# Starting the expert tiles of a routed feed-forward layer while the last rows are still being routed

## What is computed

```python
x = x + tanh(g_xattn[0]) * xattn(ctx_2048, layernorm(x), mask, mask, ...)   # 8 heads of 16
x = x + tanh(g_ffn[0])   * ffn(layernorm(x), ...)
# ffn:
scores = sigmoid(x_flat @ gate.T + bias)             # 2048 tokens x 9 experts
top_scores, selected = top_k(scores, 2)
top_scores = top_scores / (sum(top_scores) + 1e-20)
for e in range(9):
    h = silu(x_flat @ ew1[e].T) * (x_flat @ ew3[e].T)  # 352 hidden
    out = out + cw[:, e:e + 1] * (h @ ew2[e].T)
```

## Time and profile before

| | us |
|---|---|
| median of three runs | 274.59 |
| the profiled execution, its own time | 274.52 |
| its span (first to last instruction) | 272.7 |
| PE busy / DVE / ACT / POOL | 189.9 / 175.5 / 133.8 / 116.7 |

### The profile page before, as it was taken

One profiled execution on the slowest core, in us unless ns is written; L12 is line 12 of the kernel. 1 busy time (PEld: TensorE's weight loads), 2 busy tenths in 40 slices (PEclk: granted clock), 3 DMA queues, 4 the chain that ended last, 5 costly groups with the idle time before them and its releaser, 6 DMA issues.

```text
span 272.7 us, 5842 instructions
## 1 busy us (share of the span) xinstructions
PE 189.9 (70%) x1480; PEld 158.4 (58%) x1481; DVE 175.5 (64%) x681; ACT 133.8 (49%) x383; POOL 116.7 (43%) x196
## 2 busy tenths in 40 slices
PE   0399988989887878766300005999999999999300
PEld 0377745666555645453200004999999999998200
DVE  2248875787998779677685911566776677676125
ACT  1355539888867667573570101355455445544000
POOL 3315741332314651761377700156555655555400
PEclk9999999999999799975555555799999999999955
DMA  5904400094000010180012203022222222220096
GB/s 186 303 20 123 110 0 2 5 324 161 4 1 21 30 33 0 39 287 16 5 54 79 88 20 79 2 54 61 60 62 64 59 52 64 65 56 33 0 257 204
DMA packets 23718, 21.02 MB, mean 77 GB/s; under 512 B 3520, under 2 KB 19844, under 8 KB 23696
## 3 DMA queue, kind: packets, MB, share of 16 engines
q1 hardware_dynamic: 19152, 15.67, 19.8%
q0 software_dynamic: 2432, 4.30, 4.9%
q10 hardware_dynamic: 2112, 0.80, 1.2%
HBM read 14.81 MB, written 6.47 MB: 78 GB/s over the span
## 4 chain that ended last, share of the span: by engine, by line
PE 50%; DVE 21%; issue 9%; DMA 8%; SPq 6%; POOL 3%; ACT 2%; another core or an unknown queue 0%; DVEq 0%; POOLq 0%; ACTq 0%
PE ps_b L1007 10%; PE score_ps L975 5%; PE score_ps L976 5%; PE score_ps L977 5%; DVE mx L672 5%; PE score_ps L831 3%; PE pt_ps L1017 3%; DMA mask_b<-in_mask 3%; PE ps_b L940 3%; PE score_ps L841 3%; DMA w<-y_rows 3%; PE ps_a L919 2%; POOL x_rows L490 2%; PE ps_a L990 2%; DVE st L737 2%
## 5 line engine op out<-in xcount | busy, mean ns | idle before, releaser
L505 POOL DMA_INDIRECT y_rows<-probsT,ids x40 | 39.7, 992 | 11.1 <-POOL ids L503 11.1
L333 ACT ACTIVATE probs<-score_ps,less 128x128 f32<-128x128 f32 x128 | 37.1, 394 | 2.4 <-DVE less L676 2.4
L490 POOL DMA_INDIRECT x_rows<-stage,slot x32 | 33.5, 1047 | 9.8 <-issue 8.6
L1007 PE MATMUL ps_b<-w,probsT 128*128 (+1 forms) x240 | 33.4, 275 | 1.1 <-DVE probsT L808 1.1
L420 ACT COPY probsT<-pt_ps 128x256 f32<-128x256 f32 x40 | 14.9, 372 | 37.1 <-PE pt_ps L1017 31.6
L1007 PEld LDWEIGHTS ps_b<-w,probsT 128*128 128x128 f32 (+1 forms) x240 | 31.6, 190 | 1.7 <-issue 1.6
L484 POOL TENSOR_TENSOR rs<-ve,minus_half 128x1 f32<-128x1 f32 x16 | 9.0, 564 | 53.2 <-DVE ve L742 41.2
L793 DVE TENSOR_TENSOR probs<-probs,score_ps 128x352 f32<-128x352 f32 x40 | 20.9, 522 | 16.9 <-issue 11.5
L975 PE MATMUL score_ps<-w_high,xg_low 128*128 x80 | 30.5, 382 | 0.0
L990 PE MATMUL ps_a<-cst,xg 128*128 128x128 f32 x40 | 11.6, 289 | 26.7 <-DMA xg<-x_rows 25.9
L976 PE MATMUL score_ps<-w_low,xg_high 128*128 x80 | 26.6, 333 | 0.0
(11 more groups left out here) (149 smaller groups left out, 463.4 us busy)
## 6 DMA issues: line engine op xcount, KB each, us to landing
w<-in_w13T SPq DMA_DIRECT2D x3, 1056.0 KB, 8.4
xg<-x_rows SPq DMA_DIRECT2D x40, 65.0 KB
ctx_r<-in_ctxT SPq DMA_DIRECT2D x4, 512.0 KB, 5.0
w<-y_rows SPq DMA_DIRECT2D x8, 256.0 KB, 6.3
w<-in_w2T SPq DMA_DIRECT2D x1, 1728.0 KB
mask_b<-in_mask SPq DMA_DIRECT2D x4, 256.0 KB, 6.2
out<-xs SPq DMA_DIRECT2D x4, 256.0 KB, 3.3
xs<-in_x SPq DMA_DIRECT2D x3, 256.0 KB, 8.8
```

What stands on the lines that cost most here:

```text
L333: last = nc.scalar.activation(probs[:, r % 2, h, :], score_ps[:, r % 2, h, :], ACT.Exp, bias=less[:, r % 2, h:h + 1], scale=SCALE)
L490: pool.indirect_dma_start(x_rows[:, :], bass.IndirectOffsetOnAxis(ap=slot[:, c, p:p + 1], axis=0), stage[:, c, p, :], None, bounds_check=l ...
L505: pool.indirect_dma_start(y_rows[:, :], bass.IndirectOffsetOnAxis(ap=ids[:, r:r + 1], axis=0), yt[:, r, :], None, bounds_check=last_row, o ...
L1007: last = nc.tensor.matmul(bank[7][:, 0:D], hidT[0:cn, q3, c, :], w2[0:cn, bass.ds(e3, 1), c, :].rearrange("p o d -> p (o d)"), start=(c == ...
```

## The change

The numbers in the constants: 40 tiles are now handed out in three parts, `TILES` = 8, 8 and 24. A part is worked out from the rows placed so far: parts 0 and 1 hold only tiles whose 128 rows are all there (after two and after three groups), part 2 the rest.

- `turns` ends after step 16. The end of the attention chain of blocks 14 and 15 and the routing of groups 2 and 3 go between the first eleven tile steps (`between`), on each engine by a list of its own. The first sixteen tile steps are written out.
- The first eight tiles wait for the scatters of groups 0 and 1 only, the next eight for group 2, the rest for group 3. The table is made three times (`table_counts`, `table_rows`, and `table_used`, which takes away the tiles already given).
- A group's scatters are spread: two in step 4g+10, two in 4g+11, four in 4g+12.
- The pads are no longer aimed: all of `x_rows` (19,584 rows of 520 B, 10.2 MB) is filled with pads by one DMA ahead of the scatters, issued on SP behind the weights.
- The first-layer weights are loaded in the projections, into `w13_low`; ACT rounds them to `w13_high` there (seven of nine; two in steps 0 and 1), and DVE subtracts in place, two in the projections and one in each of steps 0 to 6.
- `maxima` is one reduction with its sign turned; the scale moves into `head_rows`. The four blocks' logits stand side by side in PSUM and are read once per group. The second layernorm writes straight into `stage` (with `scalar_tensor_tensor`), POOL makes the second copy (`keep`) and adds the epsilon; ACT no longer copies rows. The residual is kept in place, without a copy.
- In the tiles ACT takes over the weighing of the result, and copies the three transposed pieces at once; DVE keeps `xg_low`, the product and the row numbers. A place in `xg` comes free when the result is made (`y_done`), no longer when it has landed.
- `y_rows` is laid out by token, up to 4 KB in a row per partition for a load; it comes in five pieces, the last two of half size, and so do the stores.
- `consts` has 776 columns in place of 464.

```diff
+PARTS = [slice(0, 4), slice(4, 8), slice(8, 12), slice(12, 14), slice(14, 16)]
...
 CAP = NB * P + P
+EARLY = (TR, TR)
+TILES = EARLY + (NT - sum(EARLY),)
...
-
-            for k in range(NB + 2 * UN):
+        def turns(step):
+
+            for k in range(NB + 1):
...
-        def tile_turns(eng, step):
-
-            for k in range(TR):
-                step(k, k, 0)
-            with eng.Fori(1, NT // TR) as i:
+            return b >= n
+
+        def tile_turns(eng, step, between):
+
+            for k in range(sum(EARLY)):
+                step(k, k % TR, k // TR)
+                between(k)
+            with eng.Fori(sum(EARLY) // TR, NT // TR) as i:
                 for r in range(TR):
                     step(i * TR + r, r, i)
             for k in range(NT, NT + 3):
...
+                if j >= 1:
+                    n = j - 1
+                    sp.dma_start(w13_low[:, 3 * n:3 * n + 3].bitcast(F32), w13T[3 * n:3 * n + 3].rearrange("e p a b -> p e a b")).then_inc(ld_w13[n], 16)
+            sp.wait_ge(pad_set, 2)
+            sp.dma_start(x_rows[NE * CAP:NE * CAP + P], pads[:, 0, :]).then_inc(st_pad, 16)
+            sp.dma_start(x_rows[0:NE * CAP].rearrange("(p n r) w -> p n (r w)", p=P, r=NE),
+                         pads[:].rearrange("p r w -> p (r w)").unsqueeze(1).to_broadcast([P, CAP // P, NE * RW])).then_inc(st_pad, 16)
             sp.wait_ge(scores, 2 * UN + 1)
-            for n in range(NE // 3):
-                sp.dma_start(w13[:, 3 * n:3 * n + 3], w13T[3 * n:3 * n + 3].rearrange("e p a b -> p e a b")).then_inc(ld_w13[n], 16)
-
-            sp.wait_ge(scores, 2 * NB)
             sp.dma_start(w2[:], w2T.rearrange("e p a b -> p e a b")).then_inc(ld_w2, 16)
...
-
-            sp.wait_ge(pads_known, 1)
-            for e in range(0, NE, 2):
-                at = sp.value_load(pad_at[0:1, e:e + 1], min_val=e * CAP, max_val=e * CAP + NB * P)
-                sp.dma_start(x_rows[bass.ds(at, P), :], pad_row[:]).then_inc(st_pad, 16)
-            sp.wait_ge(rows_known, 1)
-            rows = [sp.value_load(row_of[0:1, r:r + 1], min_val=0, max_val=NE * CAP) for r in range(TR)]
-            sp.wait_ge(st_pad, NE * 16)
+            for n in range(len(EARLY)):
+                sp.wait_ge(rows_known, n + 1)
+                for p in range(UN):
+                    sp.wait_ge(st_rows[p], (NG - len(EARLY) + n) * 32)
+                for r in range(TR):
+                    if n >= 1:
+                        sp.wait_ge(ids_cast, (n - 1) * TR + r + 1)
+                        sp.wait_ge(y_done, (n - 1) * TR + r + 1)
+                    row = sp.value_load(row_of[0:1, n * TR + r:n * TR + r + 1], min_val=0, max_val=NE * CAP)
+                    sp.dma_start(xg[:, r, :], x_rows[bass.ds(row, P), :]).then_inc(ld_tile[r], 16)
+            sp.wait_ge(rows_known, len(TILES))
             for p in range(UN):
-                sp.wait_ge(st_rows[p], NG * 32 + 16)
-            for r in range(TR):
-                sp.dma_start(xg[:, r, :], x_rows[bass.ds(rows[r], P), :]).then_inc(ld_tile[r], 16)
...
                 for r in range(TR):
-                    sp.wait_ge(st_y[r], i * 16)
+                    sp.wait_ge(ids_cast, i * TR + (r + 1 - TR))
+                    sp.wait_ge(y_done, i * TR + (r + 1 - TR))
                     row = sp.value_load(row_of[0:1, bass.ds(i * TR + r, 1)], min_val=0, max_val=NE * CAP)
                     sp.dma_start(xg[:, r, :], x_rows[bass.ds(row, P), :]).then_inc(ld_tile[r], 16)
...
-            y_tok = y_rows.rearrange("(c b t) d -> t c b d", c=2, t=P)
-            for g in range(NG):
-                for c in range(2):
-                    sp.dma_start(ys[:, c, g * UN:(g + 1) * UN, :], y_tok[:, c, g * UN:(g + 1) * UN, :]).then_inc(ld_y[g][c], 16)
-            for g in range(NG):
+            y_tok = y_rows.rearrange("(t b c) d -> t b c d", t=P, c=2)
+            for g, here in enumerate(PARTS):
+                sp.dma_start(ys[:, here, :, :], y_tok[:, here, :, :]).then_inc(ld_y[g], 16)
...
+            def high(e):
+
+                act.wait_ge(ld_w13[e // 3], 16)
+                nc.scalar.copy(w13_high[:, e], w13_low[:, e].bitcast(F32)).then_inc(w_high, 1)
...
+                for e in ((), (0, 1), (2, 3), (4, 5, 6))[j]:
+                    high(e)
...
+                if k < 2:
+                    high(7 + k)
+                if routed(k, r, 6) is not None:
+                    sigmoid_exps(routed(k, r, 6))
...
+                if has(k, 3):
+                    t, place = k - 3, (r - 3) % TR
+                    turn = i if r >= 3 else i - 1
+                    act.wait_ge(y_mm, t + 1)
+                    if not isinstance(k, int) or t >= TR:
+                        act.wait_ge(st_y[place], turn * 16)
+                    nc.scalar.activation(yt[:, place, :], bank[5][:, 0:D], ACT.Copy, scale=xg[:, place, C_WEIGHT:C_WEIGHT + 1]).then_inc(y_done, 1)
...
+                    nc.scalar.copy(hidT[:, q, :, :], bank[4][:, 0:NC * P].rearrange("p (c t) -> p c t", c=NC)).then_inc(hid_copied, 1)
+            def between(k):
+
+                if k == 0:
+                    turned_back(NB + 1)
+                    nc.scalar.preload_act_table(ACT.Silu)
+                if k == 2:
+                    turned_back(NB + 2)
+                if k == 4:
+                    sigmoid_exps(NG - 1)
+                    nc.scalar.preload_act_table(ACT.Silu)
+
+            tile_turns(act, tile, between)
...
+                    rstd2_of(k - 3)
+                for p in range(UN):
+                    if routed(k, r, 2 * UN + 2 + min(p, 2)) is not None:
+                        scatter(routed(k, r, 2 * UN + 2 + min(p, 2)), p)
+                if on(k, 3):
+                    keep(k - 3)
+
+            def keep(b):
+
+                par, place = b // UN % 2, b % UN
+                pool.wait_ge(ln2, b + 1)
+                nc.gpsimd.tensor_copy(stage[:, par, 1, place, 0:D], stage[:, par, 0, place, 0:D]).then_inc(kept, 1)
...
+            def scatter(g, p):
+
+                par = g % 2
+                pool.wait_ge(label_set, g + 1)
+                if g == 0 and p == 0:
+                    pool.wait_ge(st_pad, 2 * 16)
+                pool.wait_ge(kept, g * UN + p + 1)
+                for c in range(2):
+                    pool.indirect_dma_start(x_rows[:, :], bass.IndirectOffsetOnAxis(ap=slot[:, par, c, p:p + 1], axis=0), stage[:, par, c, p, :], None,
+                                            bounds_check=last_slot, oob_is_err=False).then_inc(st_rows[p], 16)
...
+            rstd2_of(NB - 2)
+            keep(NB - 2)
+            rstd2_of(NB - 1)
+            scatter(NG - 2, 0)
+            scatter(NG - 2, 1)
+            keep(NB - 1)
+            scatter(NG - 2, 2)
+            scatter(NG - 2, 3)
             for k in range(NT):
                 tile(k, k % TR)
+                if k == 5:
+                    for p in range(UN):
+                        scatter(NG - 1, p)
...
+            def low(e):
+
+                dve.wait_ge(w_high, e + 1)
+                nc.vector.tensor_tensor(w13_low[:, e], w13_low[:, e].bitcast(F32), w13_high[:, e].bitcast(F32), ALU.subtract).then_inc(w_low, 1)
...
+                if j >= 2:
+                    low(j - 2)
...
+
+                nc.vector.tensor_scalar(stage[:, g % 2, :, :, C_ID], part["first_ids"].rearrange("p (c b) -> p c b", c=2), 2.0 * UN * g, None, ALU.add)
+                nc.vector.tensor_copy(slot[:, g % 2], slot_f[:]).then_inc(label_set, 1)
...
-                nc.vector.tensor_reduce(mx[:, r % 2, here], score_ps[:, r % 2, here, :], AX.X, ALU.max).then_inc(maxed, 1)
-                dve.wait_ge(maxed, 2 * k + half + 1)
-                if after(k, 2):
-                    dve.wait_ge(prob, 2 * k - 2)
-                nc.vector.tensor_scalar(less[:, r % 2, here], mx[:, r % 2, here], -SCALE, None, ALU.mult).then_inc(lessened, 1)
...
+                nc.vector.tensor_reduce(less[:, r % 2, here], score_ps[:, r % 2, here, :], AX.X, ALU.max, negate=True).then_inc(lessened, 1)
...
+                nc.vector.scalar_tensor_tensor(stage[:, par, 0, place, 0:D], xs[:, b, :], mv2[:, q, 0:1], rs2[:, q:q + 1].to_broadcast([P, D]),
+                                               ALU.subtract, ALU.mult).then_inc(ln2, 1)
...
+                if 2 + k < NE:
+                    low(2 + k)
...
+                if k == 3 * UN + 2:
+                    table_counts(0)
+                if k == 3 * UN + 3:
+                    table_rows(0)
+                if k == 3 * UN + 4:
+                    table_used(0)
...
+            def table_counts(n):
+
+                tiles, first, by_expert = table_span(n)
...
+            def between(k):
+
+                if k == 0:
+                    norm2(NB - 2)
+                if k == 1:
+                    dve.wait_ge(o_mm, NB)
+                    keep_ranks(NG - 2)
...
+                    weigh(NG - 2)
+                    place_rows(NG - 2)
+                    label_rows(NG - 2)
+                if k == 2:
```

(44 more changed lines are left out.)

495 lines of the change are left out of this document (233 added, 262 removed).

## The result

The changed kernel takes 262.98 us (median of 4 runs, 261.73 to 264.55) against 275.12 us for the kernel before (4 runs, 274.15 to 276.5): a ratio of 0.956, 95% interval 0.948 to 0.963. It is faster, by 12 us, where 25.5 were forecast, and it lies outside the range of 240 to 260. The profiled execution took 264.55 us, its span 262.7.

What follows compares the result with a forecast made beforehand. Bound: a cross-engine chain in a 45.0 us gap before the first tile, then PE at 2.07 us a tile. 274.5 + 0.5 + 1.5 - 1.7 - 34.4 + 11.0 - 2.4 = 249.0 us, range 240 to 260.

Steps and rivals of the forecast that it cites:

- What bounds the kernel, and the start of the tiles: Step 16 to first tile: chain of scatters, landing, value load and load, 10.6 us in place of 45.0; -34.4.
- Tile steps: Tile steps 0 to 10: DVE the bound with 29.3 us of work, 34.8 in all with stalls; +11.0.
- surcharge of a scatter step: Attention steps beside scatters: step 10 cost 1.7 us over a quiet step; mostly kept and spread as 0.7, 0.7 and 1.4.
- Steps 11 to 42 are PE's, as before: Later tile steps: PE stays the bound at 2.07 us each, ACT well below that.
- Steps 3 to 15: Attention steps: 70.05 us against 71.75, from dropping `less`, less table parts and spread scatters; -1.7.
- rival 1: Attention steps: scatters cost less, surcharge and late root go, -5 to 244.0; one of rivals 1 and 2 0.17, both 0.08.
- The turned sign: Attention steps: `less` and its issue leave the path between maximum and `rden`, 0.3 us a step, thirteen times, 3.9.
- Start: Ahead of step 3: larger `consts` +0.5 us, weights' rounding and subtraction on ACT and DVE +1.5 (0 to 3.2).
- Tables of ACT: Tile steps 0 and 4: three table loads, 3.9 us, the first perhaps hidden; drains, 4.1 more, left out.
- Pads and end: Fill of 10.2 MB hidden ahead of first scatter at about 87; end from 16.6 to 14.2 us, -2.4.
- rival 4: Tile 16 waits for POOL, whose stores of six tiles come first: 253 us; chance 0.05.
- Rival 3, the clock: Early tiles: clock stays at half, a tile takes 3.2 us for 2.07; 253 to 257, up to 258; chance 0.20.

Runs made afterwards that it cites:

- the chip without the delay: Chip of the first series: changed kernel with scatters of groups 0 and 1 two a step took 242.1 us there, kernel before 263.43.
- the four-a-step run: Changed kernel with the scatters of groups 0 and 1 four in each of two steps: 259.24 us, ratio 0.944.
- first series: Changed kernel without group 3's scatters 243.01 us, POOL busy instead 245.98, scatters spread 255.93, two a step 242.1; kernel before 263.43.
- the run with POOL busy: Changed kernel with additions on POOL in place of group 3's eight scatters: 245.98 us (0.934) on one chip, 257.7 (0.942) on another.
- third series: One chip: unedited changed kernel 260.19 us, without group 3's scatters 250.78, spread 267.82, two a step 261.19; kernel before 274.92.

## Why the prediction was right and wrong

**What bounds the kernel, and the start of the tiles: right.** The chain through POOL's last four scatters, their landing, a value load and a load was forecast at 10.6 us and took 10.5. The first tile begins at 127.4 in place of 132.0 since the attention steps took 7.0 us less than forecast and began 2.5 later.

**Tile steps: the step that failed.** I costed the scatters of groups 2 and 3 as POOL's time and as landing, "10.3 us", and asked only whether tile 16's rows would be there in time. They were. What I left out is what scatters do to the others, though the earlier trace rows show it: a logit for which DVE idles 1.84 us beside a scatter (PE had it ready at 88.1, so DVE takes it 1.5 us late; in quiet steps 0.1). I called it a surcharge of a scatter step, priced it in the attention and did not carry it to the tiles, which I put beside 16 scatters in two rows of eight. There it cost 7.2 us at tile 6 (steps 4 and 5, with ACT's two table loads, took 13.8 where I had 4.3 + 2.3 = 6.6; on the chip without the delay they took 6.5, from 134.64 to 141.11) and 11.9 at tile 12. The run without group 3's scatters, on another chip, took 11.3 off that hole. Before the change these sixteen scatters, 134 to 156, stood in a hole in which PE had almost nothing to do; they were in the chain that the tiles waited for, but there was next to no matrix work beside them to hold up. "Steps 11 to 42 are PE's, as before" failed at step 11; the others took 2.14 in place of 2.07, and step 12 3.2, at a granted clock of 0.63.

Apart from the delays the early tiles were priced too dear. On the chip without the holes steps 0 to 10 took 31.1 us (121.40 to 152.54) where I had 34.8, with DVE busy for 21.7 us in them where my terms add up to 29.3. DVE was not the bound there.

**Steps 3 to 15: 7 us too dear, and 4 of them a slip of addition.** The terms that I list for them, thirteen quiet steps of 4.5, 4.2 of surcharges, 1.0 for the late root and 2 for the table, add up to 65.7 us, not to the 70.05 that went into the sum. Measured were 63.1. With 65.7 the forecast would have been 244.7 and farther off. So the total missed by 14 us only by luck: the two holes cost 19.1 us, and the attention steps paid 7.0 of it back.

Of the rest, quiet steps took 4.37, forecast 4.5, and steps 10 and 11, with two scatters each, 4.5 and 4.6 where I had 5.2. This was rival 1, and its cause is not shown. Its cast did take 0.17 us in place of 0.43, but in the changed kernel none of these casts stands beside a scatter any more; and the four-a-step run has the same DVE operations and pays 6.3 and 6.8. The surcharge goes by how many scatters stand in a row, and part of it is POOL's root behind them, which I had at 1.0 for step 13 and which on the first series' chip is a wait of 2.4. Step 12 has four and took 7.1, forecast 5.9.

The page of the Trainium skill that I named for that rival (SBUF — State Buffer, Who interferes with whom) has DVE's two-port operations and POOL's writing of descriptors shut each other out. What looks like it is small here: L632 takes 0.40 us at 140.15 beside a scatter and 0.15 in its three other turns. The large delays fell on ACT too, in waits for PE and not in the length of operations, and POOL's scatters kept their 1.28 us throughout. In the run with POOL busy, DVE's operations stretched beside POOL's additions.

**The turned sign: mis-sized.** 0.13 us a quiet step for the 0.3 of the earlier trace rows; the rest of the quiet step's gain, from 4.6 or more to 4.37, is in the other edits. No run took these apart.

**Start: within what varies.** Step 3 began 4.5 us later than before in the profiled execution, 1.5 later in the one of the third series, for the same kernel. PE's wait for masks and context beyond the first was 2.6 us in the former and 1.1 in the latter. The forecast of +2.0 lies between.

**Tables of ACT: right.** Two loads in step 4, by ACT's timeline:

```profile
149.36 1.28 ACT L378 ACT_TABLE_LOAD   x1
150.66 0.27 ACT L378 ACTIVATE sigs<-logits 128x73 f32<-128x73 f32 x1
150.94 1.28 ACT L427 ACT_TABLE_LOAD   x1
152.24 0.27 ACT L395 CAST xg_high<-ps_a 128x128 fp32r<-128x128 f32 x1
```

The next operation stands 0.02 us behind each load. The Trainium skill (ScalarE: Activation LUTs, on `ACT_TABLE_LOAD`) has a drain of about 1380 ns beside each; no row here has it, and by it the sum would have been 4.1 us higher for a reason that is not there.

**Pads and end: right.** The page has the fill of 9,945 KB landing 34.8 us behind its issue at 27.5, so at 62, 23 us ahead of the first scatter. The end took 14.6, forecast 14.2. The wait that rival 4 had at tile 16 is not there (2.1 us from tile 15 to 16).

**Rival 3, the clock,** was right in part. From 117 to 135 us it was granted 0.50, as the rival had it, though it fell before PE's wait for tile 0 and not through it, and from 136 to 142 1.00. Then it fell again in the holes (1.00 from 166.7 to 170, 0.79 to 175, 0.50 to 180.7), and that costs where PE begins again: 3.2 us from tile 12 to 13. But the holes came first.

## What to carry to other kernels

Work that delays others costs nothing in a hole and much where it is moved beside a busy pipeline. When a change fills a hole, list what else stood in the hole, and look in the trace for what that does to its neighbours, not only for how long it takes. When experiments may land on another chip, run the unedited kernel beside them. And add the terms of a sum up once more.

## What the runs showed of the hardware

- Indirect scatters issued 1.28 us apart on POOL made ACT and DVE see PE's finished work late, in order and by more with each: 2.5, 4.2, 8.5 and 11.1 us in a row of eight. At 2.3 us apart, or one in 2.07 us, there was no such delay. The other direction, PE seeing DVE, was prompt (0.14 us).
- It does not go by the rows written: eight scatters of 64 rows gave a hole of 14.5 us, of 128 rows 12.4 on the same chip. POOL busy for 8.8 us without transfers gave none. What inside the chip is held up is not shown.
- A row of four scatters costs about 2 us in an attention step even where PE's results are not late, through POOL's reciprocal root, which waits its turn behind them: 11.8 against 9.8 us for two steps.
- Chips differ. On one, the same file ran with a step of 2.5 us beside the same eight scatters and took 242.1 us, on another 11.2 us and 261.2; the kernel before took 263.4 and 274.9.
- Lengthening the code of PE by 64 instructions moved its packets away from all three rows of scatters and left the holes as they were (10.5 and 13.9 us); so did 44 more on POOL (10.0 and 11.9).
